# Two MoE and attention layers on one core: first blocks' rows in scatter passes, slot counts ahead of the last queries, accumulators closed earlier, an accumulating transfer at the end

## The reference

```python
xn = _layernorm(x)
x = x + linear_attention(xn) + routed_32_experts_top8(xn) + shared_expert(xn)
xn = _layernorm(x)
x = x + gated_linear_attention(xn) + routed_8_experts_top2(xn) + shared_expert(xn)

def body(acc, ws):                       # layer 0, once for each of 32 experts (width 176)
    wg, wu, wd, cw = ws                  # cw: weight of this expert for each token, 0 where not chosen
    h = jax.nn.silu(x @ wg.T) * (x @ wu.T)
    return (acc + cw[:, None] * (h @ wd.T), None)
```

## Time and profile before

| | |
|---|---|
| median of 3 runs | 1018.84 us (1015.52 to 1022.83) |
| the profiled execution | 1013.84 us, span 1012.0 us, so 1.84 us lie around the span |
| mean granted TensorE clock | 0.924 |
| busy share of the span | TensorE 83%, its weight loads 59%, VectorE 35%, ScalarE 31%, GpSimd 49% |
| DMA | 175.71 MB; mean 174 GB/s |

### The profile page before, as it was taken

How to read it: one execution, slowest core, us unless ns; L and a number is a source line. 1 busy time by engine, 2 the same in 40 slices (tenths; PEclk the granted TensorE clock), 3 DMA queues, 4 the chain that set the end, 5 groups by cost and what they waited for, 6 DMA issues and landing times.

```text
span 1012.0 us, 15484 instructions
## 1 busy us (share of the span) xinstructions
PE 839.7 (83%) x3786; PEld 592.4 (59%) x3786; DVE 359.2 (35%) x1047; ACT 312.7 (31%) x845; POOL 492.9 (49%) x383
## 2 busy tenths in 40 slices
PE   2969997830699998999999999950889999999960
PEld 2737754630465665666666666630856667777750
DVE  4642246720132332333333333333351353344442
ACT  4221121200233333333333333311421223354530
POOL 4017576776265665666666666541207314333320
PEclk9989998985799999999999999985599999999995
DMA  9349972442799899899988998989403415443357
GB/s 354 156 176 368 393 249 104 139 162 106 218 298 289 193 200 251 184 184 185 186 183 186 184 189 184 199 194 223 131 6 118 135 15 98 67 68 61 48 83 176
DMA packets 110402, 175.71 MB, mean 174 GB/s; under 512 B 13584, under 2 KB 82832, under 8 KB 107960
## 3 DMA queue, kind: packets, MB, share of 16 engines
q1 hardware_dynamic: 68944, 116.16, 36.6%
q0 software_dynamic: 36768, 54.39, 29.0%
q10 hardware_dynamic: 4608, 4.20, 1.7%
HBM read 94.50 MB, written 80.19 MB: 173 GB/s over the span
## 4 chain that ended last, share of the span: by engine, by line
PE 37%; POOL 27%; issue 16%; DMA 13%; DVE 4%; ACT 2%; SPq 1%; POOLq 0%; DVEq 0%; ACTq 0%
POOL accs L558 15%; POOL xg L549 12%; PE banks L847 10%; DMA accs<-yb,xb 9%; PE banks L873 7%; PE banks L832 2%; PE banks L690 2%; PE banks L858 2%; PE banks L672 2%; PE banks L714 2%; PE banks L663 1%; PE banks L615 1%; PE banks L920 1%; PE banks L624 1%; PE banks L989 1%
## 5 line engine op out<-in xcount | busy, mean ns | idle before, releaser
L558 POOL DMA_INDIRECT accs<-yb,xb x198 | 312.2, 1577 | 309.2 <-ACT yb L1128 254.9
L847 PE MATMUL banks<-wgu,xt 128*128 x636 | 234.2, 464 | 0.3 <-ACT xt L1116 0.3
L1528 DVE SCALAR_TENSOR_TENSOR hid<-sg,xb,banks 128x176 f32<-128x176 f32 x198 | 78.7, 397 | 382.7 <-ACT sg L1122 382.7
L549 POOL DMA_INDIRECT xg<-tok,slot_int x160 | 157.2, 982 | 107.5 <-issue 64.1
L873 PE MATMUL banks<-wd,ht 88*128 88x256 f32 x636 | 184.9, 384 | 11.3 <-issue 8.3
L1116 ACT COPY xt<-banks 128x256 f32<-128x256 f32 x198 | 73.8, 373 | 275.4 <-PE banks L832 275.4
L832 PE MATMUL banks<-cst,xb 128*128 128x128 f32 x396 | 108.2, 275 | 46.8 <-DMA xb<-xg 45.7
L873 PEld LDWEIGHTS banks<-wd,ht 88*128 88x128 f32 x636 | 97.1, 192 | 55.3 <-issue 39.2
L847 PEld LDWEIGHTS banks<-wgu,xt 128*128 128x128 f32 x636 | 97.3, 192 | 41.2 <-issue 26.6
L832 PEld LDWEIGHTS banks<-cst,xb 128*128 128x128 f32 x396 | 56.0, 142 | 89.2 <-DMA xb<-xg 47.1
L858 PE MATMUL banks<-cst,hid 128*88 128x128 f32 x396 | 108.1, 274 | 0.0
(11 more groups left out here) (208 smaller groups left out, 865.6 us busy)
## 6 DMA issues: line engine op xcount, KB each, us to landing
xb<-xg SPq DMA_DIRECT2D x198, 144.5 KB, 3.5
wd<-in_wdn SPq DMA_DIRECT2D x159, 176.0 KB
accs<-zeros SPq DMA_DIRECT2D x20, 544.0 KB, 12.1
xg<-blank_rows SPq DMA_DIRECT2D x7, 1156.0 KB, 18.3
wgu<-in_wgu SPq DMA_DIRECT2D x20, 352.0 KB, 6.1
accs<-yb,xb POOLq DMA_INDIRECT x198, 5.2
wgu<-in_wgu SPq DMA_DIRECT2D x1, 2816.0 KB, 26.7
gu<-in_wgu SPq DMA_DIRECT2D x1, 2816.0 KB
```

Of the source, the lines that this page charges most:

```text
L549: pool.indirect_dma_start(xg[n], bass.IndirectOffsetOnAxis(ap=(slot_int1 if n else slot_int)[:, t, k:k + 1], axis=0), tokw[:, t, :], None)\
L558: pool.indirect_dma_start(accs[a], bass.IndirectOffsetOnAxis(ap=xb[:, g % RING, ROW_ID:ROW].bitcast(U32), axis=0), yb[:, g % YB_RING, :], ...
L847: mm = pe.matmul(bank[2 + g % 2][:, 0:2 * F0], xt[:, g % 2, k, :], w[:, bass.ds(expert[g], 1), k, :].rearrange("p a n -> p (a n)"), start= ...
L1528: v.scalar_tensor_tensor(out=hb_[:, g % 2, :], in0=sg[:, g % 2, :], scalar=weight, in1=bank[2 + g % 2][:, F0:2 * F0], op0=ALU.mult, op1=AL ...
```

## The change

- **Passes.** The 128 scatters are issued with the lowest slots first: pass n is the 16 DMAs with k = 7 - n, and counts on one of two semaphores (`passes`), by n's parity. GpSimd waits for pass n-2 before pass n. VectorE works out, in `block_needs`, how many even and odd passes each of the first `CAREFUL` = 32 blocks needs by its expert's number (a token's n-th lowest expert is at least n, so expert e is complete after passes 0 to e), and writes two counts into `need`. SyncE reads both for each of these blocks and waits for those counts; block 32 on need all passes.
- **Early adds.** Pass 7 waits for the filled accumulators, and five adds (blocks 0 to 4) stand between its scatters, one after every third.
- **Rings.** `xb` has 14 buffers, loaded `AHEAD` = 6 blocks ahead; `yb` has 7.
- **Slot counts.** `slot_sums(0)` stands ahead of the last two of the eight query products.
- **Accumulators.** `LAST0` is 28, `LAST1` 12, and `CLOSED_AT` moves with `LAST0`, from 148 to 134.
- **End.** `acc` plus `fin_a` is stored to `out` at once. `fin_b` is gone: GpSimd waits for the last add and the stores, and one DMA adds the 2 MB of accumulator 5 to `out`, from DRAM to DRAM, in rows of 8 KB.

```diff
-RING, LAG = 12, 3
+RING, AHEAD = 14, 6
-WD_RING, YB_RING = 3, 4
-ACCS0, LAST0 = 4, 14
-ACCS1, LAST1 = 2, 5
+WD_RING, YB_RING = 3, 7
+ACCS0, LAST0 = 4, 28
+ACCS1, LAST1 = 2, 12
+PASS = 16 * NT
+CAREFUL = 32
+EARLY_ADDS, ADD_EVERY = 5, 3
...
             def block_rows(g):
                 n, b = layer(g)
+                if g < CAREFUL:
+                    counts = [sp.value_load(need[0:1, n_, g:g + 1], min_val=PASS, max_val=PASS * TOPK0 // 2)
+                              for n_ in range(2)]
+                    for n_ in range(2):
+                        sp.wait_ge(passes[n_], counts[n_])
+                elif g == CAREFUL:
+                    for n_ in range(2):
+                        sp.wait_ge(passes[n_], PASS * TOPK0 // 2)
                 if g >= RING:
...
-            sp.wait_ge(scattered[0], 16 * SCATTERED[0])
-            for g in range(RING):
+            sp.wait_ge(needs_known, 1)
+            for g in range(AHEAD):
                 block_rows(g)
             experts_in(1)
             for g in range(NB0):
                 if g + WD_RING < NB0:
                     down_weights(g + WD_RING)
-                if g >= LAG and g - LAG + RING < NB0:
-                    block_rows(g - LAG + RING)
+                if g + AHEAD < NB0:
+                    block_rows(g + AHEAD)
...
-            sp.wait_ge(added_to[ACCS0 + 1], 16 * adds_to(ACCS0 + 1))
-            for q in range(0, NBLK, 2):
-                rows_by_chunk(fin_b, accs[ACCS0 + 1], slice(4 * q, 4 * q + 4), fin_in[q])
...
-            for k in range(TOPK0):
+            for n in range(TOPK0):
+                if n >= 2:
+                    pool.wait_ge(passes[n % 2], PASS * (n // 2))
+                if n == TOPK0 - 1:
+                    pool.wait_ge(filled, 16 * FILLED)
+                    pool.wait_ge(acc_st, 16 * BATCH)
                 for t in range(NT):
-                    scatter_rows(0, t, k)
-            pool.wait_ge(scattered[0], 16 * SCATTERED[0])
...
+                    scatter_rows(0, t, TOPK0 - 1 - n, passes[n % 2])
+                    if n == TOPK0 - 1 and t % ADD_EVERY == ADD_EVERY - 1 and t // ADD_EVERY < EARLY_ADDS:
+                        add_rows(t // ADD_EVERY)
+            for g in range(EARLY_ADDS, NB0):
...
+            pool.wait_ge(added_to[ACCS0 + 1], 16 * adds_to(ACCS0 + 1))
+            pool.wait_ge(stored, 16 * NBLK * BATCH)
+            pool.dma_start(out.rearrange("(c r) d -> c (r d)", r=8),
+                           accs[ACCS0 + 1][0:T, :].rearrange("(c r) d -> c (r d)", r=8), accum_op=ALU.add, max_dma_last_dim=8192)\
+                .then_inc(last_added, 16)
...
                 query_product(b, 1)
-            slot_sums(0)
+                if b == 2:
+                    slot_sums(0)
...
+            def block_needs():
+                dve.wait_ge(table_done, 1)
+                e = table[0:1, 0:CAREFUL]
+                for low in (2, 4, 6):
+                    for n in range(2):
+                        at = passes_[:, n]
+                        if low == 2:
+                            last = v.tensor_scalar(at, e, float(low + n), None, ALU.is_ge)
+                        else:
+                            last = v.scalar_tensor_tensor(out=at, in0=e, scalar=float(low + n), in1=at,
+                                                          op0=ALU.is_ge, op1=ALU.add)
+                    link(last)
+                v.tensor_scalar(need[:], passes_[:], float(PASS), float(PASS), ALU.mult, ALU.add).then_inc(needs_known, 1)
...
-                last = v.tensor_tensor(acc[:, tiles], acc[:, tiles], fin_a[:, tiles], ALU.add)
-            link(last)
-            for q in range(NBLK):
-                tiles = slice(4 * q, 4 * q + 4)
-                dve.wait_ge(fin_in[q], 16 * BATCH)
-                v.tensor_tensor(acc[:, tiles], acc[:, tiles], fin_b[:, tiles], ALU.add).then_inc(fin_added, 1)
+                v.tensor_tensor(acc[:, tiles], acc[:, tiles], fin_a[:, tiles], ALU.add).then_inc(fin_added, 1)
```

More of the change, by code:

```diff
@@ L100 @@
 FILLED = FILLS * (ACCS0 + ACCS1 - 1) + 1
-SCATTERED = (NT * TOPK0, NT * TOPK1)
+SCATTERED = NT * TOPK1
+PASS = 16 * NT
+CAREFUL = 32
+EARLY_ADDS, ADD_EVERY = 5, 3
 TABLE_AT = 2
@@ L143, in build @@
         RING_AT = W_AT + E0 * EXPERT_BYTES
-        SUMS_AT = RING_AT + 13888
+        SUMS_AT = RING_AT + 16192
         BUF_AT = SUMS_AT + 33024
         BESIDE_AT = BUF_AT + 6144
-        SMALL_AT = BESIDE_AT + 11264
+        SMALL_AT = BESIDE_AT + 14080
         main = region(ACC_AT, RING_AT)
@@ L178, in build @@
         table = small("table", [1, COLS0], I32)
+        need = small("need", [1, 2, CAREFUL], I32)
         table1 = small("table1", [1, COLS1], I32)
@@ L220, in build @@
         over = early("over", [P, E0, NT])
+        passes_ = early("passes_", [1, 2, CAREFUL])
         a_nat = early("a_nat", [P, 4, D])
@@ L231, in build @@
         fin_a = first("fin_a", [P, NT, D])
-        fin_b = region(W_AT, W_AT + 16384)("fin_b", [P, NT, D])
         dense1 = region(SUMS_AT, BUF_AT)
@@ L289, in build @@
         ends_blank = sem("ends_blank")
-        scattered = [sem(f"scattered{n}") for n in range(2)]
+        passes = [sem(f"passes{n}") for n in range(2)]
+        scattered = sem("scattered")
+        needs_known = sem("needs_known")
         acc_st = sem("acc_st")
@@ L300, in build @@
         fin_early = sem("fin_early")
-        fin_in = [sem(f"fin_in{q}") for q in range(NBLK)]
+        last_added = sem("last_added")
         stored = sem("stored")
@@ L507, in _ @@
             sp.dma_start(dn1[:], wdn1).then_inc(gu1_in, 16)
-            sp.wait_ge(scattered[1], 16 * SCATTERED[1])
+            sp.wait_ge(scattered, 16 * SCATTERED)
             for g in range(NB0, ALL_BLOCKS):
@@ L546, in _, with scatter_rows @@
                     .then_inc(bo_added, 1)
-            def scatter_rows(n, t, k):
+            def scatter_rows(n, t, k, done):
                 pool.indirect_dma_start(xg[n], bass.IndirectOffsetOnAxis(
-                    ap=(slot_int1 if n else slot_int)[:, t, k:k + 1], axis=0), tokw[:, t, :], None)\
-                    .then_inc(scattered[n], 16)
+                    ap=(slot_int1 if n else slot_int)[:, t, k:k + 1], axis=0), tokw[:, t, :], None).then_inc(done, 16)
             def add_rows(g):
@@ L570, in _ @@
             pool.wait_ge(placed, 1)
-            for k in range(TOPK0):
-                for t in range(NT):
-                    scatter_rows(0, t, k)
-            pool.wait_ge(scattered[0], 16 * SCATTERED[0])
-            v.tensor_copy(tok_id, cst[:, C_NAT1:C_NAT1 + NT]).then_inc(ids_made, 1)
-            pool.wait_ge(filled, 16 * FILLED)
-            pool.wait_ge(acc_st, 16 * BATCH)
-            for g in range(NB0):
+            for n in range(TOPK0):
[4 more added lines that the diff above has]
+                    pool.wait_ge(acc_st, 16 * BATCH)
+                for t in range(NT):
+                    scatter_rows(0, t, TOPK0 - 1 - n, passes[n % 2])
+                    if n == TOPK0 - 1 and t % ADD_EVERY == ADD_EVERY - 1 and t // ADD_EVERY < EARLY_ADDS:
+                        add_rows(t // ADD_EVERY)
+            for g in range(EARLY_ADDS, NB0):
+                if g == CAREFUL:
+                    for n in range(2):
+                        pool.wait_ge(passes[n], PASS * TOPK0 // 2)
+                    v.tensor_copy(tok_id, cst[:, C_NAT1:C_NAT1 + NT]).then_inc(ids_made, 1)
                 add_rows(g)
@@ L591, in _ @@
                 for t in range(NT):
-                    scatter_rows(1, t, k)
+                    scatter_rows(1, t, k, scattered)
             for g in range(NB0, ALL_BLOCKS):
                 add_rows(g)
+            pool.wait_ge(added_to[ACCS0 + 1], 16 * adds_to(ACCS0 + 1))
[3 more added lines that the diff above has]
+                .then_inc(last_added, 16)
+            pool.wait_ge(last_added, 16)
         @block.tensor
@@ L1231, in _ @@
                 block_back(NB0 + n, NB0, ALL_BLOCKS)
-            act.wait_ge(added_to[ACCS0 + 1], 16 * adds_to(ACCS0 + 1))
-            for q in range(1, NBLK, 2):
-                rows_by_chunk(fin_b, accs[ACCS0 + 1], slice(4 * q, 4 * q + 4), fin_in[q])
             for q in range(1, NBLK, 2):
@@ L1400, in beside_tile0 @@
                     expert_table(0)
+                if t == TABLE_AT + 1:
+                    block_needs()
             for c in range(NBLK):
```

1 line of the change is left out of this document (removed).

## The result

The changed kernel takes 1005.72 us (median of 4 runs, 1003.46 to 1010.48) against 1017.46 us (4 runs beside it, 1015.52 to 1022.83): a ratio of 0.9898, 95% interval 0.9864 to 0.9932. It is faster by 1.0%, some 10 us, where 25 us were forecast. The profiled execution has a span of 1001.7 us, 10.3 under the 1012.0 of before, so its stages can be set against the sum.

A forecast was written before the change was run, and what follows sets the result against it. It saw TensorE idle 45.73 us awaiting the scatters, then setting a 2.50 us block pace until adds fell behind. Terms -26 + 1.4 + 3 - 3.5 = -25.1 us gave median 994, forecast 985 to 1003, outer range 976 to 1008.

The forecast's parts named there:

- a part of that, or a last transfer of 21 us: Rival: part of the slowdown from two accumulators in layer 0's last 28 adds, or slower end transfer; 1001 to 1009, chance 0.10.
- Slot counts, 3.4 us: Front part: counts moved ahead of two query products, so scatters start and the front part ends 3.4 us earlier.
- First blocks, 26 us won: Start of layer 0: blocks don't wait for all scatters; SyncE's 3.6 us turns put block 28's add at 318.7, against 344.62.
- the adds' own limit: Early layer 0: adds from block 5 wait for the last scatter (261), so block 28 could come at 308, hidden under SyncE's limit.
- The rival that reads cost nothing: First blocks: SyncE's register reads run ahead of its waits, so the adds' limit decides; 983 us, chance 0.18.
- Accumulators closed at block 131, 1.4 us lost: End of layer 0: last 28 adds alternate between two accumulators, eight beside the sums' loads at 3.5 us; 1.4 us lost.
- TensorE is not stopped: Last 28 adds of layer 0: seven `yb` buffers allow 17.5 us of lag, so late adds don't stop TensorE.
- The rival "slower": Last 28 adds of layer 0: all landings take 7.3 us, an add costs 4.0, `yb` stops TensorE; 1021 us, chance 0.04.
- Layer 1, 3 us lost: Layer 1's last twelve adds on one accumulator, 4.63 us apart, plus 2 us beside stores; landing at 996.2 for 993.2.
- Last transfer, 3.5 us won: End of the kernel: the accumulating transfer takes 15 us, with 0.3 ahead, replacing 18.8 us; 3.5 us won.
- The rival with a plain load's 8.5 us: End of the kernel: the last transfer goes at a plain load's rate, 8.5 us; 987 us, chance 0.14.

## Why the prediction was wrong, and where it was right

The forecast was 25.1 us of gain; the profiled execution shows 10.3. The median, 1005.72, lies inside the outer range (976 to 1008), but in the part that belonged to the rival "a part of that, or a last transfer of 21 us" (1001 to 1009), which had a chance of 0.10. Its first half is what happened. The 14.8 us between forecast and measurement are, by the prediction's terms, 2.9 (first blocks), 3.6 (not in the sum), 8.0 (accumulators 0 and 1), -0.7 (layer 1) and 1.0 (last transfer):

- **Slot counts, 3.4 us:** right. The first scatter started 3.6 us earlier (73.86 for 77.48). First rows were issued at 213.31 (said: 213.2), the first down-weights at 226.24 (225.8).
- **First blocks, 26 us won:** 23.1, 2.9 less. SyncE's pace was right: 3.6 us a turn, and turn 25 issued its weights at 313.63 (said: 313.6). TensorE waited for `xb` (21 waits, 26.8 us, from 214 to 320), not for `wd` as said: the size was right with the wrong operand. By the code a block's rows are turned ahead of the down product of three blocks earlier, so 6 rows ahead are no more than 3 weights ahead. With 9 ahead (and `LAST0` = 14) the wait moves to the matmuls on the down-weights (13 waits, 15.5 us), and block 28 comes no more than 3.5 us earlier, so that the pace is SyncE's with either. Without the reads it comes at 305.67, where the adds' own limit was put at 308. The last scatter was issued at 251.61, not 261: four pauses of GpSimd among the scatters of the kernel before (7.24, 2.74, 2.38 and 2.46 us, with no releaser in the trace) are gone, for a cause not looked into. The rival that reads cost nothing is refuted: they cost 15.9 us at block 28.
- **Not in the sum, 3.6 us lost:** near block 43 loads of layer 1's weights (704, 384 and 512 KB) fall among rows that are only 6 ahead. Rows land in up to 8.3 us there, at a share of 1.08 from 359 to 363 us. TensorE idled 3.31 us, up to 362.31, and the granted clock was 0.60 over the 8 us from 360, that is mostly the lower level of 1.2 GHz. The loss varies: 2.9 to 10.3 us in eight kernels with rows 6 ahead. With rows 9 ahead it is 4.7 at most, 1.1 with AHEAD = 9 alone.
- **Accumulators closed at block 131, 1.4 us lost: this is the step that failed.** It was 9.4. The price of an add beside the loads was taken at 3.5 us, halfway to what a landing of 7.3 us gives, and those 7.3 us are from a stretch (660 to 672 us) in which SyncE issued no rows any more. Beside rows and weights an add lands in 8.0 us and the next comes 4.4 us later; over all 28 the adds are 3.3 us apart (said: 2.95). And "TensorE is not stopped" rested on the `yb` buffers alone. It stopped for rows (10.3 us), which land over the same full engines (7.7 us for 3.5) and are issued by the same queue, whose turn grew to 3.8 us with four more transfers in it. The prediction priced SyncE's turn at the start and left it out here. The rival "slower" named this very collision (loads 14 blocks earlier at a share of 0.90) with a landing of 7.3 us; what kept it small is that it ends with the 4.2 MB. The experiments show the place as the cause: with the loads late and rows 9 ahead the tail is 13.4 us, that of before. They show the bytes at 6 to 7 us in either place, which before pays too in all likelihood; that the rest of the difference is SyncE's turns is argued from the queue and not shown by a run.
- **Layer 1, 3 us lost:** 2.3 (10.1 us ahead at the last add of layer 0; the last add of all lands at 985.4 for 993.2, 7.8 ahead). The size is right, with its parts shifted. The eleven adds are 4.7 us apart, about as said, but from the add that meets `fin_a`'s load to the next it is 9.5 us (922.76 to 932.23) where 12.9 were taken, so the last add starts 10.5 us ahead. The stores then make its landing 6.5 us, 2.8 more than before (said: 2 for the last two adds).
- **Last transfer, 3.5 us won:** 2.5 from the last landing (16.3 us to the end for 18.8). The transfer took 12.8 us (said: 15). What the sum left out is that it does not start when the last add has landed, but when `out` is stored: GpSimd issues it at 987.36, 1.9 us after the landing. The two terms together, from the last add of layer 0 to the end, come to 0.2 us won (said: 0.5). Counted from the last add's start the new end gains nothing: either end moves twice 2.1 MB over engines that are nearly full (0.97 and 0.90 before, 0.87 and 0.94 now), and fewer stores changed nothing. The rival with a plain load's 8.5 us is refuted. The Trainium skill's fit for a DMA issued by GpSimd ("DMA: Bandwidth & Descriptors", section Anatomy of one DMA, SWDGE path), 2.0 us plus bytes / 436e3, estimated 6.8 us here; the trace doesn't agree, with 12.8.

## What to carry to other kernels

Where the DMA engines are at 0.9, a transfer moved earlier isn't free just because the adds have slack: ask what else has to land, and be issued, beside it, and look at which loads run fewest blocks ahead, since they stop the engine first. Moving the next one further ahead only hands the stop on (here from rows to down weights). Count ahead-distances from where an operand is first read in the engine's order, not from the block's number. And an instruction queue that issues for everyone is a budget per block, wherever in the program it is spent: four more issues a turn made eight turns 9 to 10 us too long. Two register reads of 0.74 us with each of 32 row loads cost 13 to 18 us, and dropping one of the two gave all of that back.

## What was unexpected of the hardware

- A DRAM-to-DRAM accumulating transfer of 2.1 MB in rows of 8 KB ran at 184 GB/s with a DMA share of 0.94. In two halves, each over a view with one more dimension, it ran at 99 and 98 GB/s with a share of 0.50, in two kernels. That half of the engines carried it would fit; which ones did was not looked at, and no other form of the view was tried. The view's outermost dimension, 4 long where the single transfer's is 256, is the first thing to change.
- With the engines full (1.03 to 1.11), transfers on which nothing was changed slow down too: rows go from 3.5 to 7.7 us, adds from 5.2 to 8.0.
- Not of the hardware: with rows 9 ahead the trace names no releaser for the waits before the down product (9.0 us in the tail). That they are for the down weights follows from the code's other two waits having been over.
